# Second attention of a two-layer decoder: output product ahead of the next transposes, and values placed in their own pass

## The reference

```python
x = x + _L0_xattn_ref(_layernorm(x), ctx_4096, wq, wk, wv, wo)      # 32 heads of 128
x = x + _L0_ffn_ref(_layernorm(x), W0, bias0, W1, bias1)            # fp8 quantised
x = x + _L1_xattn_ref(_layernorm(x), ctx_4096, ctx_4096, Wq, Wk, Wv, Wo)
x = x + _L1_ffn_ref(_layernorm(x), weight, bias, centroids, assignments)
...
def _L1_xattn_ref(query, key, value, Wq, Wk, Wv, Wo):               # 32 heads of 16, 8 kv heads
    q = (query @ Wq) ; k = repeat(key @ Wk, 4) ; v = repeat(value @ Wv, 4)
    probs = softmax(q k^T * 16 ** -0.5)                             # over the 64 tokens of a sequence
    return (probs @ v) @ Wo
```

## Time and profile before

| | us |
|---|---|
| median of 3 runs | 1602.65 |
| lowest and highest | 1600.28, 1606.68 |
| the profiled execution | 1601.44 |
| its span, first to last instruction | 1599.7 |
| TensorE, VectorE, ScalarE, GpSimd busy in the span | 1481.6, 1257.5, 845.3, 303.5 |
| loop of attention1 in the trace | about 1356 to 1530 |

### The profile page before, as it was taken

The page is one execution under the profiler, slowest core; times in us unless marked ns, Lnnn a source line. Parts: engine busy times, 40 slices in busy tenths (PEclk is TensorE's granted clock), DMA queues, the critical chain, the costliest instruction groups (busy, mean ns, idle before and its releaser), DMA issues. The chain is left out here.

```text
span 1599.7 us, 29290 instructions
## 1 busy us (share of the span) xinstructions
PE 1481.6 (93%) x11214; PEld 779.1 (49%) x11214; DVE 1257.5 (79%) x2249; ACT 845.3 (53%) x1773; POOL 303.5 (19%) x271
## 2 busy tenths in 40 slices
PE   6999999999999999999999987799999998678678
PEld 3555555555555555555555443344444445344344
DVE  4878876677777777677777787988888885999877
ACT  3554562343433433433424432688888863888742
POOL 0032130011111102010111100011111102789730
PEclk9999999999999999999999998999999999999889
DMA  6276573214331231414132232132223350776502
GB/s 250 80 175 169 139 179 79 80 54 106 65 93 53 60 110 28 121 47 118 52 105 57 49 119 94 50 47 47 47 52 58 63 100 1 146 106 111 104 1 106
DMA packets 317163, 140.77 MB, mean 88 GB/s; under 512 B 265873, under 2 KB 290577, under 8 KB 316818
## 3 DMA queue, kind: packets, MB, share of 16 engines
q1 hardware_dynamic: 273954, 98.15, 28.5%
q10 hardware_dynamic: 43120, 41.42, 8.3%
HBM read 66.13 MB, written 11.53 MB: 49 GB/s over the span
## 5 line engine op out<-in xcount | busy, mean ns | idle before, releaser
L639 PE MATMUL xp<-WO,OT 128*128 128x512 f16 x1536 | 344.2, 385 | 7.8 <-DVE X L924 7.8
L600 PE MATMUL pj<-XT,WQ 128*128 128x512 f16 x1536 | 340.4, 381 | 5.5 <-DVE WQ L285 4.9
L639 PEld LDWEIGHTS xp<-WO,OT 128*128 128x128 f16 x1536 | 149.1, 99 | 194.1 <-issue 24.8
L600 PEld LDWEIGHTS pj<-XT,WQ 128*128 128x128 f16 x1536 | 148.6, 98 | 182.5 <-issue 9.0
L757 ACT ACTIVATE E<-E 128x512 f32<-128x512 f32 x64 | 40.2, 628 | 292.2 <-DVE E L902 292.2
L1163 PE MATMUL db<-W0T,XD 128*128 128x448 f16 x768 | 155.4, 361 | 10.6 <-ACT db L1263 7.4
L1181 PE MATMUL eb<-W1T,DT 128*128 128x512 f16 x672 | 149.0, 381 | 3.9 <-ACT eb L1273 3.9
L924 DVE SCALAR_TENSOR_TENSOR X<-xp,X 128x512 f32<-128x512 f32 x128 | 88.2, 689 | 78.4 <-PE xp L639 77.3
L574 POOL TENSOR_TENSOR VW<-VW,XB 128x1024 f32<-128x1024 f32 x14 | 33.0, 2357 | 601.9 <-DVE VW L103 601.9
L862 DVE SCALAR_TENSOR_TENSOR QT<-pj,QT 128x512 f16<-128x512 f32 x128 | 88.0, 687 | 70.4 <-ACT QT L727 70.4
L1163 PEld LDWEIGHTS db<-W0T,XD 128*128 128x128 f16 x768 | 75.1, 100 | 87.8 <-ACT db L1263 13.0
(11 more groups left out here) (240 smaller groups left out, 2433.8 us busy)
## 6 DMA issues: line engine op xcount, KB each, us to landing
W0T<-in_L_xattn_wo ACTq DMA_DIRECT2D x15, 1024.0 KB, 5.3
W0T<-in_L_xattn_wq SPq DMA_DIRECT2D x9, 1024.0 KB, 5.4
W0T<-in_L_xattn_wq ACTq DMA_DIRECT2D x7, 1024.0 KB, 6.2
X<-in_x SPq DMA_DIRECT2D x4, 1024.0 KB, 7.5
XB<-in_L_ffn_W ACTq DMA_DIRECT2D x28, 128.0 KB, 3.0
w0t<-XB ACTq DMA_DIRECT2D x7, 512.0 KB, 7.5
w1t<-W0T ACTq DMA_DIRECT2D x7, 512.0 KB, 7.7
W0T<-w0t ACTq DMA_DIRECT2D x1, 3584.0 KB, 11.7
```

Source lines behind the costliest of these rows:

```text
L600: last = pe.matmul(bank[:, :], w, src[:, b, k, tokens], start=n == 0, stop=n == 3 * KC - 1)
L639: last = pe.matmul(xp[i % 2][:, :], OT[:, a, j, i * P:(i + 1) * P], WO[:, b, j, :], start=n == 0, stop=n == 3 * REP - 1)
```

## The change

```diff
@@ TensorE, pass t
                 if t + REP < UNITS:
                     project(t + REP)
+                if t >= 2:
+                    project_out(t - 2)
                 if t + AHEAD < TILES:
                     transposes(t + AHEAD)
                 if t in W_SLOT:
                     turn_weights(W_SLOT[t])
-                if t >= 2:
-                    project_out(t - 2)
                 if 1 <= t <= TILES:
                     weigh_values(t - 1)
@@ ScalarE
-            place_values(0)
             for t in range(TILES + 3):
...
                 if t == TILES:
                     stats_scalar(act, 3, (0,))
-                if t + 1 < TILES:
-                    place_values(t + 1)
+                if t < TILES:
+                    place_values(t)
```

## The result

The changed kernel took 1607.76 us (median of 20 runs, 1602.87 to 1611.48) against 1602.46 us of the kernel before in the same comparison (20 runs). The ratio is 1.0035, with a 95% interval from 1.0027 to 1.0044: 5.6 us slower by the ratio, 5.3 by the two medians. The forecast was 1607.0 and its sum +4.5 us; the range and the case "within 0.5%" hold.

A forecast was written before the change was run, and what follows sets the result against it. VectorE's work was taken to bound each loop pass, with TensorE's product late by 0.52 us. Terms -3.1, 0, +1.1 and +6.5 gave +4.5 us: 1605.9, or 1607 us on the median's footing, range 1600.5 to 1612.

The forecast's parts named there:

- within 0.5%: Whole kernel: the time stays the same, neither 1594.6 us or less nor 1610.7 or more; chance 0.74.
- The bound: Second attention's loop: VectorE's own work sets the pass, and TensorE's late product costs it 0.52 us a pass.
- Part 1: Passes 2 to 7, output product ahead of the tile's transposes: each pass 0.52 us shorter, 3.1 us gained.
- Part 2: ScalarE's placement one slot later in the program: 0 by itself; the new one in pass 15 priced with Part 4.
- Part 3: Passes 12 to 15, output product ahead of the weight transposes: +1.1 us, from pass 13 at half clock, otherwise 0.
- Part 4: Pass 16, the tail: VectorE's low half of the last weights waits behind the output product, +6.5 us; +4.0 at full clock.
- Late transposes (2): Rival, passes 2 to 7: ScalarE's copy slips behind the later transposes, Part 1 gives nothing; +7.6 us, 1610.2; 8%.
- ScalarE as the bound (4): Rival: ScalarE's 7.9 us of waits come off and the tail costs nothing; 1594.7 us; 4%.
- Full clock in passes 13 and 16 (1): Rival: TensorE at full clock in passes 13 and 16; 0.0 in sum, 1602.6 us; 15%.
- Half clock in 13, 14, 15 and 16 (3): Rival: TensorE at half clock in passes 13, 14 and 15 as well as 16; +8.5 us, 1611.1; 19%.

The follow-up runs named there:

- e1: Kernel before, with only TensorE's output product moved ahead of the tile's transposes in passes 2 to 7: ratio 0.9979, -3.4 us.
- e2: Kernel before, with only ScalarE's value placement moved one slot later, into its own pass: ratio 1.0022, +3.5 us.
- e10: The same kernel as e2, run once more against the kernel before: ratio 1.0009.
- e9: The edit of e2 on the kernel before, but ScalarE's placement still waits for TensorE's weighing of the same pass: ratio 0.9996.
- e6: Kernel before, with only the output product moved ahead of the weight transposes in passes 12 to 15, not 16: ratio 1.0015, +2.4 us.
- e4: Kernel before, with only the output product moved ahead of the weight transposes in pass 16 alone: ratio 1.0033, +5.3 us.
- e3: Kernel before, with only the output product moved ahead of the weight transposes in passes 12 to 16: ratio 1.0048, +7.7 us.
- e8: The changed kernel, with VectorE's first statistics ahead of the last weights' low half in pass 16: ratio 1.0017 against the kernel before.
- e5: Kernel before with the edits of e1 and e2 together, weight transposes still ahead of the product: ratio 0.9993, -1.1 us.

## Why the prediction was right, point by point

**The bound.** VectorE was late by TensorE's weighing, 0.52 us a pass, and ScalarE's longer wait was not on the path. Right: e1 alone shortens the passes to 9.66 us, e2 alone leaves them at 10.18.

**Part 1, -3.1 us.** Right in mechanism, and in size within the interval of e1 (-3.4 us, from -5.8 to -1.1). The profiles put it lower. In the changed kernel passes 2 to 7 gave 2.5 us, since the half clock fell into the projection of pass 3 (10.34 us), and each of the six profiles with this order has one such pass. The forecast had no term for it, and the seven other profiles have no such projection in these passes. What the order changes ahead of it is this: with the transposes behind the product, TensorE's two waits of a pass, 1.24 us ahead of the spread and 0.93 ahead of the transposes, became one ahead of the spread, 1.84 us in passes 3, 6 and 7 of the changed kernel and 1.73 in pass 5. That this longer wait is what makes the clock fall is not shown. (The waits of the kernel before are those of its passes 3 to 7.) That the transposes wait for the copy of bank rt and not for GpSimd's tile, as their row names it, shows in e2: in its pass 3 the projection came 1.2 us sooner against the maxima, GpSimd's tile was ready at 1386.27, and the transposes still began at 1387.85, 0.1 us behind the copy.

**Part 2, nothing.** As a term of the sum it is not contradicted, as a statement about the edit it did not hold. Released earlier, ScalarE moves TensorE's waits together (0.93 to 2.14 us ahead of the transposes), and in pass 3 the clock fell behind that wait: 1.4 to 3.5 us in e2 and e10 by their ratios, nothing that the ratio shows in e9, which keeps the wait. Why it fell in that pass and not in the four that have the same wait stays open. I had looked for the price of the edit on its own path and for none on TensorE's clock. In the change itself the transposes stand behind the product, so that no wait stands ahead of them in passes 2 to 7; the one ahead of the spread has grown in its place.

**Part 3, +1.1 us.** Mis-sized. e6 shows +2.4 us: two passes at half clock, 12 and 14, and not pass 13. The changed kernel has the same two (+0.60 and +1.82 us) and pass 13 back at full clock (-0.94), 1.5 us in these three; 0.7 us more in pass 9, where no order was changed. The forecast took the clock of pass 13 as a property of pass 13, from one profile. It is not: pass 13 took 9.05 to 9.25 us in all eleven profiles of the experiments too, among them e4, whose program is that of the kernel before up to pass 15. There pass 14 took 9.50 us instead, with a product of 4.45 us. So which pass meets the half clock differs between executions of the same code, and the -0.9 us that the forecast gave for a pass 13 at full clock is what this pass showed. What the weight order adds is passes 12 and 14: all four profiles that have it (the change, e3, e6, e8) are 0.6 to 1.3 us longer in pass 12 and 1.8 to 2.3 in pass 14; the others are no longer in pass 12, and in pass 14 by nothing to 1.4 us. By the Trainium skill, TensorE: Matmul & The Clock Gate, section "HAM oscillation — how this bites in real kernels", waits between bursts throttle the clock burst after burst; here the passes lengthened were two of four, which lies between the row of pass 13 and that rule. The page's case has bursts shorter than the waits between them, and here the bursts are the longer ones, so the forecast stretched the rule when it applied it to passes 14 and 15.

**Part 4, +6.5 us.** Right in mechanism, 1 us too large. The added idle time is 5.45 us (7.39 against 1.94), 5.3 in e4. The product of tile 14 took 4.24 us, not 5.30: the clock rose before its end (granted clock 0.59 from 1515 to 1517, 1.00 from 1517 to 1519). The lower bound of 4.0, at full clock, and the 6.5 at half clock hold it between them.

**Sum.** Run alone, the parts give -3.4 (e1) and +7.7 us (e3), +4.3 together, and +1.4 to +3.5 (e10, e2) for the placement; the change gave +5.6. That is additive within the intervals. Against the forecast of +4.5, in the lengths of the stage, the tail came out about 1 us lower and the half clock in other passes (3, 9, 12 and 14) some 1.7 us higher. The two misses have opposite signs, so part of the closeness of the sum is luck.

**The rivals.** Late transposes (2): one pass of six shows it, pass 3, where the copy for low_x waited 0.68 us for the transposes behind the half-clock projection; at full clock the margin held. ScalarE as the bound (4): fallen with e1 and e2. Full clock in passes 13 and 16 (1): half of it came, pass 13 at full clock, but others took its place. Half clock in 13, 14, 15 and 16 (3): two such passes occurred, at +5.6 us, not the +8.5 of the full case.

## What to carry to other kernels

A loop that overlaps tiles has a steady part and an end, and one exchange of two steps can help the one and hurt the other: here 3.4 us gained in six passes, 5.3 lost in one. Write the order for each part by itself, and ask in the last pass which engine still has ready work behind a wait; moving that work ahead of the wait gave back 2.9 us of the change's 5.6 (e8), and undoing the weight order gave back all of it (e5). A wait that is off the path may not be free to remove when that joins TensorE's idle times into one (e2, e10): look at the waits ahead of its bursts afterwards. And a term that rests on which pass of one profile met the half clock is worth no more than that profile.

## What the runs showed of the hardware that I had not expected

The length of TensorE's wait does not by itself tell whether the lower clock follows. In the changed kernel the products after waits of 2.10 and 2.16 us took 4.45 and 5.14 us, the one after 1.11 took 2.76. Yet the one of pass 16, after 1.10, took 4.24; in pass 13 before, 1.13 us was followed by 5.30, and in passes 4 to 7 of e2 waits of 2.13 to 2.24 us ahead of the transposes by products of 2.75. The same kernel run twice (e2, e10) had the drop in the same pass, 3, though the stage started at 1354.07 in one and at 1358.46 in the other. But the changed kernel and e8, the same program up to pass 15, had it in passes 3 and 9 in one and in pass 4 in the other.

Short instructions of VectorE lasted until one of GpSimd's had ended. In the kernel before:

```profile
1512.31 1.27 POOL L1576 TENSOR_TENSOR X<-X,VW 128x512 f32<-128x512 f32 x1
...
1512.73 1.12 DVE L1902 TENSOR_SCALAR W0T<-W0T,cid 64x512 f16<-64x512 int32 x1
```

and in the changed one:

```profile
1533.93 1.26 POOL L1576 TENSOR_TENSOR X<-X,VW 128x512 f32<-128x512 f32 x1 [4.85 <-ACT VW L1824]
...
1534.20 1.02 DVE L163 TENSOR_TENSOR ln_work<-guess 128x4 f32<-128x4 f32 x1
...
1535.25 0.16 DVE L164 TENSOR_TENSOR ln_work<-ln_work,var_eps 128x4 f32<-128x4 f32 x1
```

The one-hot instruction took 1.12 us beside GpSimd's sum and 0.47 without it; a 128x4 instruction took 1.02 us and ended 0.03 us after that sum, its neighbour of the same shape 0.16. The other profiles repeat it. The one-hot instruction took 1.11 or 1.12 us in the six of all thirteen profiles where it started at most 0.45 us behind GpSimd's sum, 0.68 in e5, where it started 0.87 us behind it, and 0.47 in the six others, where no such sum ran beside it; in the first seven it ended about 0.28 us after the sum. No run was made to test it; it moved the tail of the changed kernel by some 0.6 us either way.
